# Layer 1 of a two-layer gated cross-attention model: q3 before the attend, the exponential after the third group, POOL's normalise next to its weigh

## What is computed

```python
x = x + tanh(g_xattn[1]) * L1_xattn(layernorm(x), ctx)
x = x + tanh(g_ffn[1]) * L1_ffn(layernorm(x))

# L1_xattn: q, k, v by head; weights = softmax(q k / 8); ctx = weights v; times Wo
# L1_ffn, for each token x:
d2 = x2 + p2 - 2.0 * (x @ prototypes.T)          # 32 prototypes
w = softmax(-sqrt(d2)); topw, topi = top_k(w, 2); topw = topw / sum(topw)
out = sum over the two of topw * (A[topi] @ (B[topi] @ x) + bias[topi])   # rank 16
```

## Time and profile before

| | |
|---|---|
| median of 3 runs | 3049.57 us (3042.84 to 3050.61) |
| profiled execution | 3044.48 us, span 3042.8 us |
| PE busy | 2739.6 us, 90% of the span |
| DVE busy | 2507.4 us, 82% |
| POOL busy | 2089.8 us, 69% |
| ACT busy | 1983.7 us, 65% |
| mean granted clock of PE | 0.981 of full speed |

### The profile page before, as it was taken

The page is one execution under the profiler, slowest core; times in us unless marked ns, Lnnn a source line. Parts: engine busy times, 40 slices in busy tenths (PEclk is TensorE's granted clock), DMA queues, the critical chain, the costliest instruction groups (busy, mean ns, idle before and its releaser), DMA issues.

```text
span 3042.8 us, 96434 instructions
## 1 busy us (share of the span) xinstructions
PE 2739.6 (90%) x31534; PEld 2166.8 (71%) x31534; DVE 2507.4 (82%) x6126; ACT 1983.7 (65%) x4683; POOL 2089.8 (69%) x2777
## 2 busy tenths in 40 slices
PE   4888896899999999689699999999989999999996
PEld 2444444677777777557578888888878888888885
DVE  6877776688888888675689999899989989999885
ACT  2666666687777877575466666666656666666663
POOL 3893000567666676544388888888888888888886
PEclk9999998899999999899899999999999999999998
DMA  5987566223233232631567766666776767766663
GB/s 152 364 337 294 235 254 256 76 81 93 77 90 84 80 93 76 220 117 41 121 142 158 158 147 149 140 145 150 145 137 149 141 144 149 147 150 145 145 132 78
DMA packets 638943, 455.55 MB, mean 150 GB/s; under 512 B 389760, under 2 KB 612592, under 8 KB 633648
## 3 DMA queue, kind: packets, MB, share of 16 engines
q1 hardware_dynamic: 618288, 402.31, 52.2%
q0 software_dynamic: 7328, 23.40, 2.5%
q10 hardware_dynamic: 12960, 25.23, 2.2%
HBM read 235.08 MB, written 148.83 MB: 126 GB/s over the span
## 4 chain that ended last, share of the span: by engine, by line
PE 32%; DVE 6%; issue 4%; POOL 3%; SPq 2%; ACT 2%; DMA 1%; DVEq 0%; POOLq 0%; ACTq 0%
PE banks L150 10%; PE banks L152 9%; PE banks L151 9%; PE banks L1416 2%; DVE a_near L1540 2%; PE banks L1401 2%; SPq L1058 1%; DVE a_probT_lo L1492 1%; ACT a_qT_hi L1234 1%; DVE a_pick L1627 1%; DVE a_rsum L1504 1%; DVE a_wtop L1567 1%; POOL a_pn L1154 1%; DMA a_xnT<-a_xn_parts 0%; DMA a_hwT<-a_hw_parts 0%
## 5 line engine op out<-in xcount | busy, mean ns | idle before, releaser
L1234 ACT ACTIVATE a_qT_hi<-banks 128x512 f16<-128x512 f32 x252 | 150.4, 597 | 540.8 <-PE banks L152 540.8
L383 POOL TENSOR_TENSOR a_probT_lo<-a_expT,a_probT_hi 128x512 f16<-128x512 f32 x256 | 291.4, 1159 | 218.5 <-ACT a_probT_hi L466 218.5
L459 ACT ACTIVATE a_expT<-banks,a_top,w_score_scale 128x512 f32<-128x512 f32 (+1 forms) x384 | 272.4, 709 | 152.5 <-PE banks L550 146.1
L1154 POOL TENSOR_TENSOR a_pn<-a_prob,a_rsum 128x1024 f32<-128x1024 f32 (+1 forms) x256 | 310.2, 1233 | 5.8 <-DVE a_rsum L1506 5.8
L150 PE MATMUL banks<-a_xnT,w_q_hi 128*128 128x256 f16 x1024 | 281.2, 275 | 15.0 <-DMA a_xnT<-a_xn_parts 13.2
L150 PE MATMUL banks<-a_vo_front,a_probT_hi 128*128 128x256 f16 x1024 | 279.8, 273 | 9.4 <-DVE a_probT_lo L1492 6.5
L152 PE MATMUL banks<-a_xnT,w_q_lo 128*128 128x256 f16 x1024 | 280.6, 274 | 0.0
L151 PE MATMUL banks<-a_xnT,w_q_hi 128*128 128x256 f16 x1024 | 280.6, 274 | 0.0
L152 PE MATMUL banks<-a_vo_front,a_probT_lo 128*128 128x256 f16 x1024 | 279.7, 273 | 0.0
L151 PE MATMUL banks<-a_vo_front,a_probT_hi 128*128 128x256 f16 x1024 | 279.6, 273 | 0.0
L1490 DVE TENSOR_TENSOR a_qT_lo<-banks,a_qT_hi 128x512 f16<-128x512 f32 x252 | 172.0, 683 | 77.9 <-ACT a_qT_hi L1234 77.7
(11 more groups left out here) (380 smaller groups left out, 10177.7 us busy)
## 6 DMA issues: line engine op xcount, KB each, us to landing
vo<-kv_vo_out SPq DMA_DIRECT2D x38, 2048.0 KB, 8.1
a_vo_front<-vo SPq DMA_DIRECT2D x128, 512.0 KB
kt<-kv_k_out ACTq DMA_DIRECT2D x9, 2560.0 KB, 14.9
a_k<-kt SPq DMA_DIRECT2D x64, 308.0 KB, 3.5
kv_raw_e<-in_L_ffn_w POOLq DMA_DIRECT2D x16, 1024.0 KB, 8.9
a_x<-in_x SPq DMA_DIRECT2D x64, 256.0 KB, 2.9
a_y<-in_x SPq DMA_DIRECT2D x64, 256.0 KB, 2.7
x<-a_y SPq DMA_DIRECT2D x64, 256.0 KB, 2.8
```

Of the source, the lines that this page charges most:

```text
L383: pool.tensor_tensor(probT[b][1][:, first:end, :], expT[b][:, first:end, :], probT[b][0][:, first:end, :], ALU.subtract).then_inc(prob_rea ...
L459: act.activation(expT[1 - h][0:rows, first:end, :], bank, ACT.Exp, bias=top[0:rows, 0:1], scale=weights["score_scale"][0:rows, 0:1]).then_ ...
L1154: last = pool.tensor_tensor(keys_of(pn[h]), e[:, :, first:end], rsum[h][:, :].unsqueeze(2).broadcast_to([P, H, end - first]), ALU.mult)
L1234: act.activation(out, bank[:, 0:cols].rearrange("p (c s) -> p c s", c=out.shape[1]), ACT.Copy, scale=scale)\
```

## The change

In layer 1 only. The fourth query product (q3) gets a place of its own, number 4, which stands in h = 1 behind the transpose of wsel and ahead of the attend on PE, behind the copy of wselT on ACT, and ahead of add_residual on DVE; the ring of banks follows. On ACT the exponential of tile t-1 and the root of the second norm move from behind the second group of probabilities to behind the third. On POOL normalise moves from behind normed_low to directly behind weigh, and weighed_low goes ahead of top_weights. No operation, wait or DMA is added or removed.

```diff
--- before.py
+++ after.py
@@ -968,7 +968,7 @@
 
     def prep_uses(h, part):
 
-        at = {(0, 2): [("q", 0)], (0, 3): [("q", 1)], (1, 0): [("q", 2)], (1, 2): [("q", 3)]}
+        at = {(0, 2): [("q", 0)], (0, 3): [("q", 1)], (1, 0): [("q", 2)], (1, 4): [("q", 3)]}
         return at.get((h, part), [])
 
     def uses(i):
@@ -984,6 +984,7 @@
             names += of(8, [("ffn", h)])
             names += of(5, [("low", h, n) for n in range(LU)])
             names += of(7, [("wselT", h)])
+            names += prep(4)
             names += of(3, [("out", h)])
             names += prep(2)
             names += prep(3)
@@ -1201,14 +1202,14 @@
                     rows_low(i + 1)
                 if live(t - 7, NT):
                     weigh(t - 7, 1 - h)
+                if live(t - 2, NT):
+                    normalise(t - 2, h, u)
+                if live(t - 7, NT):
+                    weighed_low(t - 7)
                 if live(t - 6, NT):
                     top_weights(t - 6)
-                if live(t - 7, NT):
-                    weighed_low(t - 7)
                 if live(t - 4, NT):
                     normed_low(t - 4)
-                if live(t - 2, NT):
-                    normalise(t - 2, h, u)
                 if live(t - 1, NT):
                     softmax_sums(t - 1, h, u)
 
@@ -1318,12 +1319,12 @@
                         prep(0)
                         if live(t - 4, NT):
                             norm2_log(t - 4)
-                    if g == 1 and live(t - 1, NT):
-                        need(act, scores_read, t)
-                        part = prob_of(u, h, 1)[:, :]
-                        act.activation(part, part, ACT.Exp, scale=score_scale[:, 0:1]).then_inc(exp_done, 1)
-                    if g == 1 and live(t - 4, NT):
-                        norm2_root(t - 4)
+                if live(t - 1, NT):
+                    need(act, scores_read, t)
+                    part = prob_of(u, h, 1)[:, :]
+                    act.activation(part, part, ACT.Exp, scale=score_scale[:, 0:1]).then_inc(exp_done, 1)
+                if live(t - 4, NT):
+                    norm2_root(t - 4)
                 if h == 1 and live(i + 2, NB):
                     norm_log(i + 2)
                 if live(t - 4, NT):
@@ -1351,6 +1352,7 @@
                 if live(t - 7, NT):
                     bank = full(i, ("wselT", h))
                     act.activation(wselT[:, :], bank[0:BIAS_ROWS, 0:P], ACT.Copy).then_inc(wselT_hi, 1)
+                prep(4)
                 prep(2)
                 if h == 1 and live(i + 2, NB):
                     norm_apply(i + 2, u + 2)
```

## The result

| | before | after |
|---|---|---|
| median of 4 runs | 3049.27 us (3042.84 to 3050.61) | 3086.63 us (3082.66 to 3096.7) |
| profiled execution | 3044.48 us, span 3042.8 | 3082.66 us, span 3080.9 |
| ratio, 95% interval | | 1.0133 (1.0115 to 1.015) |

The changed kernel is 37 us slower. The forecast was 3052 (3022 to 3070), no measurable change; both are missed.

A forecast was written before the change was run, and what follows sets the result against it. A ring of work through PE, DVE and POOL was taken to set the 23.60 us batch, no engine being full. 30 x (-0.01) + 32 x (+0.08) = +2.3 us on the 3049.6 median gave 3052, range 3022 to 3070.

The forecast's parts named there:

- The loop's term: 32 batches of the loop body at +0.08 us each, because SP issues its turning transfers later.
- SP's queue: SP issues in order; late turning of h = 1's weighed rows makes two batches at least 47.7 us, +0.08 a batch.
- The straight code's term: 30 batches of straight code at -0.01 us each: 23.59 us a batch against 23.60.
- the ring: POOL, DVE and PE waiting on one another around a batch; its length was forecast at 23.59 us against 23.60.
- q3's move: Fourth query product ahead of PE's attend: the scores' wait of 0.66 us a batch goes, 0.2 us gained for DVE's picks.
- r: Start of DVE's rsum of h = 0 in a batch, forecast at T+4.33.
- T: Moment PE begins to transpose the probabilities of h = 0, from which a batch's times are counted.
- The rows without their gap: POOL's row subtraction follows its softmax sums at once; closing the 0.62 us gap costs what the earlier product gives.
- Normalising next to the weighing: POOL's normalise directly behind weigh: no work removed, its being early buys nothing; the sums end at r + 9.80.
- S to r: From the end of POOL's softmax sums to DVE's rsum; forecast 2.17 us in h = 0, 1.82 in h = 1.
- Rival C: SP's queue bounds the loop body, with a 4.1 us landing: +0.58 us a batch, +19 us, 3068; chance 0.26.
- The exponential: ACT's exponential behind the third group: nothing either way; at most 0.8 us if the 5 us before POOL's sums went.

The follow-up runs named there:

- e5: Kernel before with only the fourth query product moved ahead of the attend; 3045.21 us, ratio 0.9988.
- e15: Changed kernel with the exponential and the second norm's root back behind the second group; 3078.49 us, ratio 1.0121.
- e2: Kernel before with only POOL's new order; 3079.32 us, ratio 1.0114.
- e10: Changed kernel with POOL's rows_low behind weigh instead of ahead of it; 3073.26 us, ratio 1.0095.
- e6: e1 with POOL's rows_low behind weigh instead of ahead of it; 3051.16 us, ratio 1.0014.
- e1: Changed kernel with POOL's old order put back, the fourth query product and the exponential still moved; 3062.82 us, ratio 1.0054.
- e16: Kernel before with the fourth query product moved and POOL's rows_low behind weigh; 3032.72 us, ratio 0.9970.
- e17: Kernel before with only POOL's rows_low moved behind weigh; 3041.73 us, ratio 0.9986.
- e8: Changed kernel with four of the eight back-value loads issued by ACT at the end of h = 1 instead of by SP; 3064.85 us, ratio 1.0054.
- e14: e8 with the exponential and the second norm's root back behind the second group; 3056.46 us, ratio 1.0055.
- e9: Kernel before with only the exponential and the second norm's root moved behind the third group; 3058.2 us, ratio 1.0036.
- e4: Changed kernel with four of the ten value loads issued on SP behind the turnings of h = 1; 3107.69 us, ratio 1.0196.
- e11: e5 with four of the eight back-value loads issued by ACT at the end of h = 1; ratio 1.0009.
- e18: e16 with four of the value loads issued by ACT instead of SP; ratio 0.9964.

## Why the prediction was wrong

The forecast was the sum of two terms. The loop's term, 32 x (+0.08) = +2.6 us, came from SP's queue; the middle lost 27.1. The straight code's term, 30 x (-0.01) = -0.3 us, came from the ring; the two straight stretches lost 14.4. The larger miss is the loop's term.

**q3's move: right in the last stretch.** The scores' wait is gone, DVE waits for the attend by over 1 us, the picks are held, r is at T+4.34 against T+4.33. e5 bears out that it costs and gives nothing over the whole. It was priced in the last stretch alone; in the first it costs 4.4 us by itself and 6.6 in the order of the change (e15 against e2).

**The rows without their gap: right in the place, and it was the gap that hid a cost.** The one batch of before with this order was a fair guide in kind. What the hold is worth, the edit of e10 shows in four pairs: 0.38% (e10 against after), 0.40% (e6 against e1), 0.18% (e16 against e5) and 0.14% (e17).

**Normalising next to the weighing, "its being early buys nothing": this step failed.** It brings nothing, and what it gives up had a price in one stretch only. Normalise stood 4.4 us behind rsum and now stands 0.8 behind it, so POOL hangs on DVE in every half. The ring that I then closed, 21.42 + 2.17 = 23.59, had the right form; of its four terms three are met to 0.02 us. The fourth, S to r in h = 0, is 2.35: in the earlier trace rows wsel was the operation that L1161 held, here it is the picks, which end 0.25 us behind L1162, and wsel still has to follow (2733.56). That 0.2 is 2.3 of the 4.0 us that the last stretch lost; the rest stands mostly in two batches, one with 3.36 from S to r and one with 10.27 from r to S. And the ring was only closed for the last stretch. In the first one DVE has more to do ahead of rsum, and q3's move adds to it; the same POOL path of 9.8 us on top of it gives 24.8. POOL's order alone (e2) loses 4.6 us in the first stretch and 3.3 in the last. The prediction set 30 straight batches at -0.01; they lost 0.87 in the first stretch and 0.33 in the last.

**SP's queue: the chain was right, its terms were mis-sized.** This is the larger failure. Forecast 47.7 us for two batches, +0.08 a batch; measured 49.6 in the mean, +0.82 a batch in the middle. The issue of a_hwT came at T+24.6, forecast T+24.5. Its landing took 3.6 us in the mean, where the forecast had put in the median of before, 3.1; PE's first matmul came 0.3 us behind that, and from it to the T that ends the two batches it took 21.1 us in place of 20.1. The forecast took the price of PE's wait as the wait alone, without the clock that falls behind the longer ones: 21.47 us behind 2.56, 20.13 behind 1.60. It also worked out the shortest that two batches can be and took that for their length. Rival C was this mechanism: it set +19 us on the loop, where 27.1 were measured, with a landing of 4.1, without the clock and with nothing for the straight code. e8 shows that SP's queue accounts for 0.8% of the time (1.0133 to 1.0054), some 24 us. POOL's order is the larger part of what sets it off: PE's wait for a_hwT in the middle is 4.7 us before, 17.8 with q3's move alone (e5, a middle that is 3.4 us shorter all the same), 34.1 with POOL's order alone (e2) and 43.5 with all.

**The exponential, "nothing either way": right inside this change, wrong alone.** e14 against e8 shows no cost; e9 shows 0.36%. The cover that the step named was the 5 us to POOL's sums. What was late in e9 was ACT's copies for POOL, which the step did not price; in the change POOL's new order seems to cover them.

**The sum.** SP's queue 0.79% (after against e8) and 0.55% for what is left (e14, where the straight stretches lose 13.8 us and the middle nothing), together 1.34% where 1.33% was measured. Since e14 and e8 agree, this splits the loss and does not test it. Within the 0.55%, in stretches of single executions, POOL's order alone loses 4.6 + 3.3 us (e2), and q3's move on top of it 6.6 + 0.3 (e15 against e2). The exponential adds nothing that can be measured. How q3's move and POOL's order work on each other in the first stretch is read from one timeline and stays in part open.

## What to carry to other kernels

When a step is moved towards its producer, price the slack that it loses: look for how long it lay behind its input in the old order, for every stretch of the program, not only for the fastest. On a queue that issues in order, ask what stands behind the step that gets later; moving single issues within that queue hands the lateness on (e4), moving them to another queue ended it where that queue was the bound (e8) and gave nothing where it was not (e11, e18). Behind PE's wait of 2.56 us the clock was at half for some 3.4 us, so a late landing can cost more than the wait.

## What the runs showed of the hardware

DVE's picks, near, wsel and wtop, standing beside a POOL operation, were held to about POOL's end, and several in a row can each be held: one batch of the loop body showed the two picks at 1.79 us in place of 0.51, a steady one of the last stretch wtop at 0.47 and the picks at 1.31. The Trainium skill, "SBUF — State Buffer", section "Who interferes with whom", says that the second is blocked for the whole instruction; the traces agree, and the sum over a stretch shows as DVE's busy time, 251 to 263 us for the same 757 to 758 instructions. Not every operation of DVE was held: rsum, a reduction, took 0.39 to 0.42 us each of the 117 times between 1500 and 2900 us of before.

The transfer that turns a_hwT took 3.0 to 4.5 us to land in 300 us of the changed loop body, median 3.3 (before 3.0 to 5.1, median 3.1). What makes single ones late isn't shown. Ten loads of values held SP's queue for 9.8 us in the batch shown, and four of them took mostly 3.85 us of ACT's queue in e8. PE's granted clock fell to 1.2 GHz after it had stood for 2.56 us, and was back at 2.4 GHz in the window from 2446.00; behind waits of 1.60 and 1.92 us (until 2491.69 and 2516.14) it stayed at 1.00.
